# Taking the similarities of 24 of 32 batches, and the first average, out of the hand-over between two stages

## What is computed

```python
x = _layernorm(x + _L0_attn_ref(x, wq, wk, wv, wo))      # attention, 32 heads, 8 key heads, times W_o
x = _layernorm(x + _L0_xattn_ref(x, ctx, weight))        # below
x = _layernorm(x + _L0_ffn_ref(x, A, B, Wr, br))         # eight gated low-rank products

def _cosine_sim(a, b):                                   # over the rows of a batch
    na = jnp.maximum(jnp.sqrt(jnp.sum(a * a, axis=1)), EPS)
    nb = jnp.maximum(jnp.sqrt(jnp.sum(b * b, axis=1)), EPS)
    return jnp.sum(a * b, axis=1) / (na * nb)
sim = jnp.stack([_cosine_sim(embedding, emb_l), _cosine_sim(embedding, embedding),
                 _cosine_sim(embedding, emb_r)], axis=1)
att = jnp.repeat(sim, C, axis=1)
out = jnp.einsum('bit,oi->bot', inp_unf * att, w_flat)   # a convolution with 3 taps over columns
```

## Time and profile before

| | |
|---|---|
| median of 3 runs | 1395.52 us (1393.52 to 1397.04) |
| the profiled execution | 1392.16 us, of which its span is 1390.1 |
| TensorE (PE) busy | 1355.7 us, 98% |
| DVE, POOL, ACT busy | 79%, 70%, 67% |
| granted clock, mean | 0.992 of 2.4 GHz |
| stage two begins | 760.6 us after the start of the span |

### The profile page before, as it was taken

How to read it: one execution, slowest core, us unless ns; L and a number is a source line. 1 busy time by engine, 2 the same in 40 slices (tenths; PEclk the granted TensorE clock), 3 DMA queues, 4 the chain that set the end, 5 groups by cost and what they waited for, 6 DMA issues and landing times. The chain is left out here.

```text
span 1390.1 us, 32350 instructions
## 1 busy us (share of the span) xinstructions
PE 1355.7 (98%) x8306; PEld 1056.5 (76%) x8306; DVE 1095.9 (79%) x3873; ACT 927.2 (67%) x3262; POOL 979.0 (70%) x932
## 2 busy tenths in 40 slices
PE   8999999999999999999986999999999999999996
PEld 6777777777777777777764788888888888888884
DVE  6877787878778777878785688878887788877877
ACT  5887878878888887878785455545554455545544
POOL 4877777777777776777775677667776677767762
PEclk9999999999999999999998999999999999999999
DMA  7354545445453545445468866676665766666652
GB/s 266 100 160 116 159 116 161 121 146 149 121 161 115 165 115 152 132 134 159 131 201 242 185 159 166 157 174 153 161 156 164 172 152 165 156 169 157 161 122 76
DMA packets 109005, 213.03 MB, mean 153 GB/s; under 512 B 26656, under 2 KB 32288, under 8 KB 108960
## 3 DMA queue, kind: packets, MB, share of 16 engines
q1 hardware_dynamic: 108336, 211.46, 56.5%
q10 hardware_dynamic: 624, 1.05, 0.2%
HBM read 131.83 MB, written 34.47 MB: 120 GB/s over the span
## 5 line engine op out<-in xcount | busy, mean ns | idle before, releaser
L483 PE MATMUL wo_ps<-weights,halves 128*128 128x512 f32 x2304 | 569.7, 399 | 3.0 <-DVE weights L685 2.9
L483 PEld LDWEIGHTS wo_ps<-weights,halves 128*128 128x128 f32 x2304 | 421.5, 188 | 138.0 <-issue 53.3
L769 ACT ACTIVATE pexp<-sm,smin 128x128 f32<-128x128 f32 x1024 | 398.1, 391 | 100.6 <-DVE smin L622 99.7
L1197 PE MATMUL wo_ps<-weights,halves 128*128 128x512 f32 x1464 | 368.2, 399 | 4.3 <-PEq L145 4.3
L915 POOL TENSOR_TENSOR pn<-pexp,prec 128x512 f32<-128x512 f32 x256 | 266.7, 1047 | 98.5 <-DVE prec L629 98.5
L1667 POOL TENSOR_TENSOR prods<-prod,prods 128x512 fp32r<-128x512 f32 x186 | 251.6, 1360 | 119.9 <-ACT prods L1528 114.9
L1197 PEld LDWEIGHTS wo_ps<-weights,halves 128*128 128x128 f32 x1464 | 270.3, 189 | 62.6 <-issue 5.2
L622 DVE CUSTOM_DVE_ANT_0 sm<-s_ps,mask_t 128x128 f32<-128x128 f32 x1024 | 231.9, 282 | 26.1 <-PE s_ps L513 20.9
L1528 ACT CAST prods<-prod 128x512 fp32r<-128x512 f32 x189 | 117.1, 620 | 181.0 <-DVE prod L1380 146.7
L769 ACT ACTIVATION_READ_ACCUMULATOR pexp<-sm,smin 128x1 f32 x1024 | 193.0, 189 | 0.0
L1380 DVE TENSOR_TENSOR prod<-att,x 128x512 f32<-128x512 f32 x189 | 185.1, 993 | 9.5 <-DMA att<-sim_scratch 7.2
(11 more groups left out here) (130 smaller groups left out, 1645.8 us busy)
## 6 DMA issues: line engine op xcount, KB each, us to landing
att<-sim_scratch SPq DMA_DIRECT2D x192, 252.0 KB
pt<-blocks SPq DMA_DIRECT2D x636, 64.0 KB, 2.0
ctx_t<-in_ctx SPq DMA_DIRECT2D x32, 576.0 KB, 5.1
raw<-in_xT SPq DMA_DIRECT2D x32, 512.0 KB, 3.8
xn<-in_x SPq DMA_DIRECT2D x32, 512.0 KB, 7.6
ot_scratch<-ot SPq DMA_DIRECT2D x63, 256.0 KB, 2.1
raw<-ot_scratch SPq DMA_DIRECT2D x31, 512.0 KB, 6.8
out<-late SPq DMA_DIRECT2D x31, 512.0 KB, 6.2
```

What stands on the lines that cost most here:

```text
L483: mm = pe.matmul(qkv_ps[(par + g) % 2][:], xs[:, par, xl, k], w_sb[:, wl, g, k], start=(k == 0 and n == 0), stop=(k == KT - 1 and n == 2))
L769: ins = nc.scalar.activation(pexp[:, c % 2, i * P:(i + 1) * P], sm[:, c % 2, i * P:(i + 1) * P], ACT.Exp, bias=smin[:, c % 2, i:i + 1], sc ...
L1197: mm = pe.matmul(wo_ps[n][:], os_t[:, par, ol, k], wo_sb[:, wl, k, n * BANK:(n + 1) * BANK], start=(k == 0 and m == 0), stop=(k == KT - 1 ...
```

## The change

The similarities of batches 0 to 23 (96 of 128 rows) are made in steps 24 to 29, in the still unused `att` as scratch, those of the last eight batches in steps 32 and 33 as before, now in 32 rows. SP issues all their stores. `att` for batch 0 is loaded whole at the end of step 30. ACT therefore takes a root in step 24 too. The reciprocal is made in two halves. In step 33 DVE makes the average of batch 0 and POOL its root; the third result is split there as well, by ACT and DVE. The first half of the last batch's result goes to `xn0` instead of `ot`. x of batch 1 is loaded in step 31 instead of 32. TAIL becomes 10, so that the loop holds steps 4 to 23 and ten steps are written out.

```diff
-    LEAD, TAIL = 4, 4
+    LEAD, TAIL = 4, 10
+    FIRST = 3 * B // 4
+    EARLY = B - 8
...
+    ot_first = xn0[:, BANK:D]
+    def sim_parts(late):
+        rows = slice(4 * FIRST, P) if late else slice(0, 4 * FIRST)
+        flat = nb if late else att[:].rearrange("p k d -> p (k d)")
...
@@ SP
-        def load_sums():
+        def load_sums(late):
+            first, count = (FIRST, B - FIRST) if late else (0, FIRST)
+            sq_sums, nb_sums = sim_parts(late)[0:2]
-            sp.wait_ge(cs_out, 16 * B)
-            sp.wait_ge(summed, B)
+            sp.wait_ge(cs_out, 16 * (B if late else EARLY))
+            sp.wait_ge(summed, B if late else EARLY)
...
+        def store_sims(late):
+            sp.wait_ge(sim_made, 2 * late + 1)
+            for n, shift in ((0, 1), (1, 1), (3, 0), (4, 0)):
+                sp.dma_start(sim_row(sim_dram, n, shift, first, count), to_right).then_inc(sim_out, 16)
+            sp.wait_ge(sim_made, 2 * late + 2)
+            sp.dma_start(sim_row(sim_dram, 2, 0, first, count), to_own).then_inc(own_out, 16)
...
+            if at_step(t, EARLY):
+                load_sums(False)
             if at_step(t, B):
-                load_sums()
+                load_sums(True)
...
             if at_step(t, LAST):
-                store_sims()
                 store_first_half(b)
-                sp.wait_ge(own_out, 16)
-                sp.wait_ge(sim_out, 16 * 6)
-                start_att(sp, att, att_in, sim_dram, 0, 0)
+                store_sims(True)
...
                 sp.dma_start(xn0[:], x[0]).then_inc(xn_in[0], 16)
-                sp.wait_ge(sq_done, B)
-                sp.dma_start(xn1[:], x[1]).then_inc(xn_in[1], 16)
...
+            if at_step(t, EARLY + 5):
+                store_sims(False)
...
+            if at_step(t, EARLY + 6):
+                sp.wait_ge(own_out, 16)
+                sp.wait_ge(sim_out, 16 * 6)
+                start_att(sp, att, att_in[0], sim_dram, 0, 0, D)
             if at_step(t, B - 1):
                 load_later(4)
+                sp.dma_start(xn1[:], x[1]).then_inc(xn_in[1], 16)
@@ DVE, in step(t, par)
+                if at_step(t, EARLY) and p == 5:
+                    bound_sums(False)
+                if at_step(t, EARLY + 1) and p == 5:
+                    invert_norms(False, 0, HALF_QD)
+                if at_step(t, EARLY + 2) and p == 5:
+                    invert_norms(False, HALF_QD, QD + 1)
+                if at_step(t, EARLY + 3) and p == 5:
+                    pair_norms(False)
+                if at_step(t, EARLY + 4) and p == 5:
+                    cosines(False)
                 if p == 5 and valid(t):
                     rotate(t, par, 1)
...
             if at_step(t, LAST):
-                invert_norms()
-                cosines()
                 add_first(1)
+                average_first()
+                invert_norms(True, 0, HALF_QD)
+                invert_norms(True, HALF_QD, QD + 1)
+                pair_norms(True)
+                cosines(True)
+                low_third_out()
@@ ACT
+                if u == 0:
+                    act.wait_ge(added0, 2)
...
                 if p == 7 and at_step(t, LAST):
-                    store_sims()
                     read_ot(b, 0)
                     high_later(9)
                     load_fourth_o()
+                    high_out(2)
+                if p == 5 and at_step(t, EARLY):
+                    take_root(False)
...
                     if p == 7:
-                        take_root()
+                        take_root(True)
@@ POOL
             if at_step(t, LAST):
                 low_out(1, 1)
+                invert_root_first()
                 low_later(9)
@@ stage two
-        load_att(0, 1)
...
-            if valid(c):
+            if valid(c) and not at_step(c, 0):
                 average(c, 0)
...
-            if at_step(t, 1):
-                high_o(2, 0)
...
-            if at_step(t, 1):
-                low_o(2, 0, 0)
-                low_o(2, 0, 1)
```

More of the change, by code:

```diff
@@ L143, in build @@
             (kept[:, 0:D // 4], kept[:, D // 4:]),
-            att, [both.enter_context(nc.semaphore(f"att_in{n}")) for n in range(2)])
+            att, [both.enter_context(nc.semaphore(f"att_in{n}")) for n in range(2)],
+            both.enter_context(nc.semaphore("own_out")),
+            both.enter_context(nc.sbuf_tensor("mv0", [P, 2], F32)),
+            both.enter_context(nc.sbuf_tensor("moments", [P, 4, 3], F32)),
+            both.enter_context(nc.sbuf_tensor("power", [P, 1], F32)),
+            [both.enter_context(nc.semaphore(n)) for n in ("averaged0", "var_done0", "rstd_done0", "shifted0")])
         with ExitStack() as ctx:
@@ L287, in part1 @@
     QD = D // 4
-    sqs, nbs, norm = nb[:, 0:QD + 1], nb[:, QD + 1:2 * QD + 1], nb[:, 2 * QD + 1:3 * QD + 2]
-    own = rot1[:, 0, 0:QD]
-    own_out = sem("own_out")
+    HALF_QD = QD // 2
     right, ot_last = kept
+    ot_first = xn0[:, BANK:D]
+    def sim_parts(late):
+        rows = slice(4 * FIRST, P) if late else slice(0, 4 * FIRST)
+        flat = nb if late else att[:].rearrange("p k d -> p (k d)")
+        sums, mults, norm = (flat[rows, n * (QD + 1):n * (QD + 1) + width]
+                             for n, width in enumerate((QD + 1, QD, QD + 1)))
+        pair = (right[rows, :], xn0[rows, 0:QD]) if late else (
+            flat[rows, 3 * (QD + 1):3 * (QD + 1) + QD], flat[rows, 4 * (QD + 1):4 * (QD + 1) + QD])
+        return sums, mults, norm, *pair
     @block.sync
@@ L683, in _, with cosines @@
+        def cosines(late):
+            sums, mults, _, to_right, to_own = sim_parts(late)
+            dve.wait_ge(cos_step, 4 * late + 3)
+            dve.tensor_tensor(to_right, to_right, mults, ALU.mult).then_inc(sim_made, 1)
+            dve.wait_ge(cos_step, 4 * late + 4)
+            dve.tensor_tensor(to_own, to_own, sums[:, 0:QD], ALU.mult).then_inc(sim_made, 1)
         for n in range(PIECES):
@@ L775, in read_ot @@
             wait(act, pv_done, after(a, NU, u + 1))
-            if not (at_step(a, B - 1) and u == 1):
-                wait(act, ot_out[u], after(a, 16, 0))
-            nc.scalar.copy(ot_last if at_step(a, B - 1) and u == 1 else ot[:, u], pv_ps[:]).then_inc(ot_read, 1)
+            if at_step(a, B - 1):
+                if u == 0:
+                    act.wait_ge(added0, 2)
+                nc.scalar.copy((ot_first, ot_last)[u], pv_ps[:]).then_inc(ot_read, 1)
+                return
+            wait(act, ot_out[u], after(a, 16, 0))
+            nc.scalar.copy(ot[:, u], pv_ps[:]).then_inc(ot_read, 1)
         def move_last_row():
@@ L1077, in part2 @@
     held = sem("held2")
-    shifted = [sem(f"shifted{n}") for n in range(3)]
+    shifted = [first_steps[3]] + [sem(f"shifted{n}") for n in range(1, 3)]
     stored = [sem("stored0"), sem("stored1")]
@@ L1369, in multiply @@
             h, k = divmod(m, TAPS)
-            if k == 0:
-                wait(dve, att_in[h], after(t, 64, 64))
+            if m == 0:
+                wait(dve, att_in[0], after(t, 64, 64))
+            elif k == 0:
+                wait(dve, att_in[1], after(t, 64, 0))
             if own_home(t, m):
```

125 lines of the change are left out of this document (71 added, 54 removed).

## The result

The change made the kernel **slower**: 1398.62 us in the median (22 runs, 1394.52 to 1401.43) beside 1394.90 of the kernel before (22 runs), a ratio of 1.0019, 95% interval 1.0012 to 1.0026. The prediction was 1390.0 us, with a range up to 1394.5.

The account below looks back on a forecast made before the run. TensorE is busy 98%, but SP's queue was taken to end stage one, idling TensorE 4.31 us. Terms -2.9 - 2.9 - 0.5 + 0.8 = -5.5 us take the median 1395.52 to 1390.0 us, range 1386 to 1394.5.

Parts of the forecast that it names:

- SP's early work: Steps 24 to 30: SP's added loads and stores delay nothing TensorE needs; 0, bounds 0 and +2 us.
- Slower: the code outside the loop: Rival, 6%: engines read six more unrolled steps as new instructions; slower only above 1.6 us a step, 1401 at 1.8.
- The clock, -2.9: Behind the border: about 1.4 us of idling keeps the full clock, 21 matmuls take 4.9 us, not 7.9; -2.9 us.
- The rival that the clock falls all the same: Behind the border the clock still drops, costing 1.6 to 2.9 us of the gain: 1392.4 us; 20%.
- Another rival: Stage one ends with SP's stores or DVE's rest; the clock goes too from 2 us idling; about 1393 us; 7%.
- The end of stage one, -2.9: At the border: ACT's copy arrives last instead of SP, TensorE starts at 757.75 instead of 760.62; -2.9 us.
- First products, -0.5: Start of stage two: small waits for att's second half go, most others stay; -0.5 us, between 0 and -1.1.
- The switch, +0.8: Step 24: ACT's Sqrt and Exp table loads with the root delay the keys' copy; +0.8 us, bounds 0 and 3.0.
- DVE's early cosines, 0: Steps 24 to 28: 0.74 to 0.9 us each, placed where DVE waits 1.44 us for TensorE; 0.
- Step 32's lighter queue, 0: Step 32: 512 KB less ahead of the last move_p(0), on which TensorE waits 3.17 us; 0, bounds 0 and -1.5.

Follow-up runs that it names:

- the first experiment: The changed kernel with the one load of att moved forward within step 30, ahead of the moves of p: 1392.97 us, 0.9982 to the kernel before.
- the experiment on the average: The changed kernel's average and third result alone, similarities of all batches at the border, four steps written out: 1396.94 us, 1.0004 to the kernel before.
- the extra matmuls: Changed kernel with att's load ahead of step 30's moves, x's cast behind the queries' copy, 12 unused matmuls before the border: 1390.61 us, 0.9962 to before.
- the version with both remedies: Changed kernel with att's load ahead of step 30's moves and x's cast behind the queries' copy: 1390.38 us, 0.9961 to the kernel before.

## Why the prediction was wrong

By its own steps:

- **"SP's early work ... I take 0, bounds 0 and +2"** is the first step that failed: about 5 us (5.2 between the changed kernel and the first experiment, 4.6 between the two with the cast moved). I gave W_o's piece 10.5 us from the start of the burst's issues and reckoned 8.9, with 12.3 as the bound at two thirds of the rate; it took 16.6. That bound had the rate about right (194 GB/s; 216 measured), but not the bytes. I put 2 MB in the way, and 3.6 MB were moved until the piece had landed: `move_v`, the moves of `pt` (6.9 us to land in place of 3.1) and stores were in the same jam. And ACT waited longer for the next piece after it (2.17 us for 0.96). The rate was taken from a window that holds other transfers; no row of before shows `att`'s kind of load under pressure. That the five stores of step 29 are free failed too: the step takes 23.54 us, ACT waits 2.84 us for x in it, and with the cast moved it is 22.33 again.
- **"Slower: the code outside the loop ... 0.06 us"** is the second. I took it as a rival with 6%, and sized it by one step. It costs 0.4 us a step, 2.6 for six. The mechanism I named, engines that read new instructions, put the price on the engines; the runs show it on a DMA that is already waited for, x's, which is issued later and lands later. Why it does is open. The row that would have warned of it was in the trace of before: ACT waits for x's transfer in 25 steps, 25.5 us in all, ahead of the queries' copy. The slower result came neither by that rival alone nor at its price of 1.6 us a step.
- **The clock, -2.9**: fell. I let the idling be 1.4 us in one piece; it was 2.42 and 0.94 in two. The rival that the clock falls all the same (20%) had this, the short wait ahead included. Another rival says that the clock goes from 2 us of idling on; no row shows such a limit. It was set between a row with 1.99 us and one with 3.17, and the clock has since fallen behind 1.28 us and 0.60 ahead of that.
- **The end of stage one, -2.9**: right in mechanism, 2.25 in size. SP is no longer last, ACT's copy is, TensorE idles 0.94 us; but the copy itself came later, since the product ahead of it waits 2.42 us for `pt`. I wrote that TensorE starts 0.8 us behind the last to arrive; that held for SP (0.80 in the experiment on the average too), but behind ACT it was 0.31. The estimate for DVE was short, too: its cosines end 7.4 us behind the last transpose, for the 5.2 reckoned. The last product (32 x 256, 0.41 us like the three before it) took 2.64 us beside a rest that POOL made from 762.50 on, in 2.44 us. SP's last store waited for it; ACT's copy still came last.
- **First products, -0.5**: the stretch to the first transposes became 1.3 us shorter, of which 0.6 are the faster matmuls (7.29 for 7.88), so 0.7 is left. Right. 0.66 and 1.13 us of waiting are still there, as forecast.
- **The switch, +0.8**: 0.80 us of TensorE's waiting in step 24, and about 1 us by the step's length. Right. By the drain that the Trainium skill (ScalarE: Activation LUTs, What ACT_TABLE_LOAD costs) adds to each switch it would be 2.8 us dearer, an estimate from that page. The trace doesn't agree: from the start of the first load to the end of the second it is 3.01 us, of which the loads and the root are 2.98.
- **DVE's early cosines, 0**: right for the changed kernel. It is 1.2 us in the versions in which POOL works beside them.
- **Step 32's lighter queue, 0**: the 3.17 us wait for `pt` is gone from the trace after, but TensorE waits 3.54 us for the copy of `ot` ahead of it and 2.18 for POOL behind it. It isn't the long wait of step 31 that does this: the versions with `att` at the border and with the extra matmuls have 2.81 and 2.39 us in step 31, and still 3.56 and 3.50 for `ot`. In the first experiment and in the version with both remedies the wait for `pt` is back (2.69 and 3.15). What decides between the two isn't shown, and nothing can be said of the queue.

My sum without the clock's term, which fell, is -2.6 us for the rest of the change. What the change is worth without its two prices has two measures. With the cast early on both sides, the first experiment against the kernel with TAIL = 10, it is 5.0 us (0.9982 against 1.0019), with some 1.7 either way. With the cast moved on both sides it is 3.1 us (0.9961 against 0.9983), with some 2.3 either way, and in that are the 1.2 us of DVE's cosines beside POOL. So 3 to 5 us. The -2.6 is at the lower end of that; whether the clock makes up the rest in most executions is open, since in the profiles of these versions it falls. That the prices don't quite add up (-5.5, with 5.2 for the burst, 2.6 for the straight code and 2.9 for the clock, would be +5.2, and +2.6 was measured) stays unexplained.

**What stays open.** Why so few bytes are moved in the time of busy DMA engines behind the `att` loads wasn't tried. Nor was a variant in which the early similarities fit into the loop. And the clock: it fell behind 0.60 and 1.28 us of idling in the run with the cast moved and the burst kept (6.65 us for 21 matmuls), and stayed up behind 1.57 and 0.96 in the one without the root (5.04). So the idling just ahead of the border doesn't decide it alone.

## What to carry to other kernels

A transfer that is moved to where "nobody waits for it" has to be priced by what stands behind it in its queue: look up the next load that an engine waits for, and give the burst its own measured rate and not that of another window. Unrolling isn't free where an engine already waits for a DMA in every step: before doing it, list the waits on DMAs, and put the work that TensorE needs ahead of the one that waits. And when two edits cancel, undo them one at a time: here a change that was 2.6 us slower held 3 to 5 us of gain.

## What the runs showed of the hardware

- Steps written out cost 0.4 us each (2.6 us for 6, 5.9 for 16) while a DMA on the path is tight, and nothing measurable for six (0.9983 against 0.9983) once it isn't. The Trainium skill (Runtime: NRT & Kernel Launch, Instruction fetch mechanics) calls this fetching mostly hidden and speaks for full unrolling; for this kernel the loop was the cheaper form.
- With the loads of `att`, a piece of W_o and moves of 64 KB under way together, the DMA engines were busy at 0.98 to 1.00 and moved 188 to 197 GB/s, and the load behind `att` on the queue landed after 14.1 us in place of 5.2. Where `att` was loaded just ahead of the moves (the first experiment, 692.7 to 702.7 us), it was 167 GB/s at a share of 0.84. The share of each kind of transfer in that isn't shown.
- TensorE starts a block 0.80 us behind SP's last DMA issue but 0.31 us behind the end of ACT's last copy.
- A product on DVE of 96 x 256 took 0.41 us, and 1.51 us where POOL made a rest of 128 x 512 beside it; one of 32 x 256 took 0.41, and 2.64 us beside a rest of 128 x 1024.
